# Attention with softmax, then a mixture of experts: PSUM banks moved from the row maxima to the scores, with another order of input chunks

## The reference

```python
x = L0_attn_x                                  # (4, 1024, 512), float32
x = layernorm(x + attention(x, wq, bq, wk, bk, wv, bv, wo, bo))   # 16 heads of 32
x = layernorm(x + ffn(x, ...))                 # 8 experts, top 2, and one shared expert

def attention(x, ...):
    q, k, v = x @ wq.T + bq, x @ wk.T + bk, x @ wv.T + bv         # split in 16 heads
    probs = softmax(q @ k.T / sqrt(32), axis=-1)                  # per batch and head, 1024 x 1024
    return (probs @ v) @ wo.T + bo
```

## Time and profile before

| | |
|---|---|
| median of three runs | 2168.53 us |
| the profiled execution | 2167.16 us |
| its span, first to last instruction | 2165.4 us |
| PE busy | 2053.6 us, 95% |
| DVE, ACT, POOL busy | 58%, 40%, 40% |
| mean granted clock of PE | 0.981 |

### The profile page before, as it was taken

The page is one execution under the profiler, slowest core; times in us unless marked ns, Lnnn a source line. Parts: engine busy times, 40 slices in busy tenths (PEclk is TensorE's granted clock), DMA queues, the critical chain, the costliest instruction groups (busy, mean ns, idle before and its releaser), DMA issues. The chain is left out here.

```text
span 2165.4 us, 29932 instructions
## 1 busy us (share of the span) xinstructions
PE 2053.6 (95%) x9636; PEld 1215.9 (56%) x9637; DVE 1265.8 (58%) x2247; ACT 866.7 (40%) x1530; POOL 869.7 (40%) x828
## 2 busy tenths in 40 slices
PE   7999899999899999899999987789999999999997
PEld 5655455555455555555555433468644444446886
DVE  5777676578676477677477753466222222224875
ACT  2265564366564266565266662321111111112332
POOL 2255564455554455655354554400011111113651
PEclk9999999999999999999999999899999999999999
DMA  5322333313333313333312302671222222224752
GB/s 165 69 50 64 84 75 88 113 37 77 84 74 83 118 31 77 91 75 80 122 28 58 79 12 93 214 282 52 85 88 87 89 94 89 87 82 148 228 179 73
DMA packets 94815, 205.90 MB, mean 95 GB/s; under 512 B 24608, under 2 KB 25120, under 8 KB 92256
## 3 DMA queue, kind: packets, MB, share of 16 engines
q1 hardware_dynamic: 83888, 168.90, 26.8%
q0 software_dynamic: 10800, 35.40, 5.9%
HBM read 113.53 MB, written 39.85 MB: 71 GB/s over the span
## 5 line engine op out<-in xcount | busy, mean ns | idle before, releaser
L852 DVE TENSOR_REDUCE max_half<-ps_side 128x1 f32<-128x512 f32 x1024 | 656.7, 682 | 235.4 <-PE ps_side L600 232.5
L768 ACT ACTIVATE probs_outer<-ps_s 128x512 f32<-128x512 f32 x629 | 365.3, 600 | 204.5 <-PE ps_s L622 173.6
L622 PE MATMUL ps_s<-kq_stack 97*128 97x512 f32 x937 | 399.2, 429 | 28.6 <-ACT probs_outer L768 21.4
L600 PE MATMUL ps_side<-kq_stack 96*128 96x512 f32 x1024 | 404.8, 404 | 2.9 <-DVE max_half L852 2.3
L622 PEld LDWEIGHTS ps_s<-kq_stack 97*128 97x128 f32 x937 | 179.4, 192 | 197.6 <-issue 98.3
L1516 PE MATMUL ps_gu<-gu_sb,xT_e 128*128 x568 | 257.7, 596 | 0.7 <-issue 0.5
L1414 POOL DMA_INDIRECT x_g<-x,who_all x71 | 67.4, 949 | 454.4 <-PE ps_t L1506 358.5
L600 PEld LDWEIGHTS ps_side<-kq_stack 96*128 96x128 f32 x1024 | 196.7, 192 | 53.0 <-DVE max_half L852 18.6
L768 ACT ACTIVATE probs_mid<-ps_s 128x512 f32<-128x512 f32 x308 | 178.4, 600 | 117.2 <-PE ps_s L622 102.2
L536 POOL TENSOR_TENSOR acc<-probs_outer,probs_mid 128x512 f32<-128x512 f32 x129 | 163.7, 1295 | 151.8 <-ACT probs_mid L768 151.8
L536 POOL TENSOR_TENSOR acc<-probs_outer 128x512 f32<-128x512 f32 x129 | 163.1, 1290 | 130.7 <-ACT probs_outer L768 130.7
(11 more groups left out here) (210 smaller groups left out, 3065.9 us busy)
## 6 DMA issues: line engine op xcount, KB each, us to landing
kq_stack<-kq SPq DMA_DIRECT2D x192, 256.0 KB, 5.1
y_slots<-y_t SPq DMA_DIRECT2D x71, 256.0 KB, 2.3
res<-inv_rows SPq DMA_DIRECT2D x128, 64.0 KB, 2.0
probs_outer<-x SPq DMA_DIRECT2D x16, 512.0 KB, 5.1
x_r<-x SPq DMA_DIRECT2D x32, 256.0 KB, 3.8
x_t<-x SPq DMA_DIRECT2D x32, 256.0 KB
gu_sb<-wgu SPq DMA_DIRECT2D x8, 1024.0 KB, 15.7
out<-gu_sb SPq DMA_DIRECT2D x32, 256.0 KB, 2.7
```

The lines of the kernel that those rows point to most:

```text
L600: nc.tensor.matmul(bank, q_stack[par][0:3 * HD, h, t * P:(t + 1) * P], k_stack[par][0:3 * HD, h, half * HALF:(half + 1) * HALF], start=Tru ...
L622: nc.tensor.matmul(out, k_stack[par][0:3 * HD + 1, h, kt * P:(kt + 1) * P], q_stack[par][0:3 * HD + 1, h, half * HALF:(half + 1) * HALF], ...
L768: nc.scalar.activation(probs(loc, h), score_bank(b, loc * HG + h)[0], ACT.Exp, scale=HD ** -0.5).then_inc(probs_ready, 1)
L852: nc.vector.reduce_max(max_half[:, u // 2, u % 2:u % 2 + 1], bank, AX.X).then_inc(side_free, 1)
```

## The change

- PSUM: pre and row units have two banks in turn in place of three. The bank that comes free (`SPARE`) is a third one for scores, from slot 3 of a batch on.
- Slots: one pre in each slot up to slot 62, with two in slot 28 only. Before they stopped after slot 60, and slots 12, 28 and 44 had two.
- The second row unit of a group (slot 63) comes behind `weighted` and `row_sums` on PE.
- Chunks of x: chunks 0 and 1 at the start of group 1 as before, chunks 2 and 3 between the transfers of `spread`, 4 and 5 at the start of group 2 ahead of `invert`, 6 and 7 behind the first `invert`. The rounding on ACT and the subtraction on POOL move to later steps, and the weights are loaded ahead of chunk 2.

```diff
-PRE_TWICE = (12, 28, 44)
-PRE_UNTIL = 61
+PRE_TWICE = (28,)
+PRE_UNTIL = 63
...
-X_HIGH = {(1, 8): 0, (1, 9): 1, (1, 10): 2, (1, 11): 3, (2, 1): 4, (2, 2): 5, (2, 4): 6, (2, 5): 7}
-X_AFTER = {(1, 9): (0,), (1, 11): (1, 2, 3), (2, 1): (4,), (2, 3): (5,), (2, 5): (6, 7)}
+X_HIGH = {(1, 8): (0, 1), (2, 0): (2,), (2, 1): (3,), (2, 4): (4,), (2, 5): (5,), (2, 7): (6,), (2, 8): (7,)}
+X_AFTER = {(1, 9): (0, 1), (2, 1): (2, 3), (2, 5): (4, 5), (2, 7): (6,), (2, 9): (7,)}
...
-SIDE_RING = 3
+SIDE_RING = 2
+SPARE, PROJ_BANK = RING + 2, RING + 3
...
+        if (g, slot) == (0, TAIL_RING - 1):
+            held[SPARE] = None
...
             def body(b, m, g, last):
-                x_chunks = g == 1 and not last
-                if x_chunks:
-                    load_x(b + 1, m + 3, range(2))
+                x_first_half, x_second_half = g == 1 and not last, g == 2 and not last
+                if x_first_half:
+                    load_x(b + 1, m + 3, (0, 1))
+                if x_second_half:
+                    load_x(b + 1, m + 2, (4, 5))
                 if g:
                     invert((b * G + g) * NHALF - 1)
+                if x_second_half:
+                    load_x(b + 1, m + 2, (6, 7))
...
-                if x_chunks:
-                    load_x(b + 1, m + 3, range(2, 4))
...
                 if not (last and g >= G - 2):
-                    spread(m + 2, g % 2, m)
+                    spread(m + 2, g % 2, m, {h: lambda i=h + 2: load_x(b + 1, m + 3, (i,))
+                                             for h in (0, 1)} if x_first_half else {})
                 if not (last and g == G - 1):
                     row(m, g, 1, last)
-                if x_chunks:
-                    load_x(b + 1, m + 3, range(4, CHUNKS))
...
+                        units = side_in(last, loc, slot)
+                        for kind, u, place in units:
+                            if kind != "row" or u == 0:
+                                side_unit(b, b * G + g, g, kind, u, place)
                         if slot == SLOTS - 1 and loc % FOLD == FOLD - 1:
...
                             row_sums(b, loc)
+                        for kind, u, place in units:
+                            if kind == "row" and u == 1:
+                                side_unit(b, b * G + g, g, kind, u, place)
```

More of the change, by code:

```diff
@@ L95, in score_banks @@
     banks, held, returned = [], {0: None, 1: None}, {}
-    proj = RING + SIDE_RING
+    proj = PROJ_BANK
     for i in range(G * STEPS * HG):
         g, slot = divmod(i - HG, STEPS * SLOTS)
+        if (g, slot) == (0, TAIL_RING - 1):
+            held[SPARE] = None
         if slot == LEND and not (last and g >= G - 2):
@@ L188, in attention @@
         ps_side = ctx.enter_context(nc.psum_tensor("ps_side", [P, TAIL_RING, HALF], F32))
-        ps_proj = ps_side[:, SIDE_RING, :]
+        ps_proj = ps_side[:, PROJ_BANK - RING, :]
         def score_bank(b, i):
@@ L246, in tail_bank @@
         def tail_bank(i):
-            return ps_side[:, (i + SIDE_RING) % TAIL_RING, :]
+            return ps_side[:, (i + TAIL_RING - 1) % TAIL_RING, :]
         def res_of(t):
@@ L311, in load_w @@
                     if g == 0:
-                        sp.wait_ge(x_split, (b + 1) * CHUNKS + 3 + sel)
+                        sp.wait_ge(x_split, (b + 1) * CHUNKS + 1 + sel)
                     elif g == 1:
@@ L323, in load_x @@
                         sp.wait_ge(w_split, 2 * (n - 1) + i + 1)
-                    elif i in (4, 5):
-                        sp.wait_ge(w_split, 2 * n + i - 3)
+                    elif i < 4:
+                        sp.wait_ge(w_split, 2 * n + i - 1)
                     else:
@@ L331, in load_x, with spread @@
                                      "a p t -> (a p) t")).then_inc(x_in[i % 2], 16)
-            def spread(n, par, m=None):
+            def spread(n, par, m=None, between={}):
                 sp.wait_ge(proj_free, PROJ * (n + 1))
@@ L343, in spread @@
                                      kq[h * HD:(h + 1) * HD, parts, :].bitcast(F32)).then_inc(stacked[h], 16)
+                    if h in between:
+                        between[h]()
             def send_rows(par, half):
@@ L617, in scores @@
                     pe.wait_ge(probs_ready, b * HEADS_B + before + 1)
-                elif bank == RING + SIDE_RING:
+                elif bank == PROJ_BANK:
                     pe.wait_ge(proj_free, PROJ * (b * G + (loc - 1) // STEPS + 3))
-                elif bank >= RING:
+                elif bank >= RING and bank != SPARE:
                     pe.wait_ge(side_free, base_of(B * G - 1))
@@ L672, in batch @@
                             scores(b, loc + 1, slot)
[L673 to L676, removed]
+                        if loc == 0 and slot < TAIL_RING - 1:
+                            pe.wait_ge(tail_free, b * TAIL + KT - (TAIL_RING - 2 - slot))
+                        units = side_in(last, loc, slot)
+                        for kind, u, place in units:
+                            if kind != "row" or u == 0:
+                                side_unit(b, b * G + g, g, kind, u, place)
                         if slot == SLOTS - 1 and loc % FOLD == FOLD - 1:
@@ L797, in batch @@
                             side_unit(b * G + g, g, kind, u, place)
-                    if (g, loc % STEPS) in X_HIGH and not last:
-                        x_part(b + 1, X_HIGH[g, loc % STEPS])
+                    for i in X_HIGH.get((g, loc % STEPS), ()) if not last else ():
+                        x_part(b + 1, i)
                     if loc % KT == KT - 1:
```

## The result

The changed kernel takes 2181.93 us (median of 6 runs, 2178.96 to 2186.17) against 2162.82 us of the kernel before (6 runs, 2160.02 to 2170.02): a ratio of 1.0085 [1.0064, 1.0106]. That is 19 us slower, inside the range of 2151 to 2192 and 6 us above the forecast of 2176.

The account below looks back on a forecast made before the run. PE, busy 95% of the span, was taken to bound the kernel. From the profiled 2167.2 us, minus 31 for late chunks, plus 39 for two maxima banks, gave 2175, or 2176 against the median; range 2151 to 2192 (8 in 10).

Parts of the forecast that it names:

- The late chunks go: Six long attention pairs in batches 0 to 2, where ACT waits for chunks of x: 31 us gained, 20 as lower end.
- What the third score bank brings: Scores waiting for ACT: beyond the six pairs little gain, as the other waits are at group ends, counted in pair 7.
- Two banks in ordinary pairs: Matmuls 0.09 us late for a bank, 0.19 us per ordinary pair; 2.2 us a group, 31 us over 14 groups.
- Pair 7: Last pair of a group, slots without proj: two banks follow DVE's pace, two pre more and one wait less, +0.37 us.
- Ahead of batch 0: Stretch before the first batch's attention, where DVE is nearly full as it is: +1.5 us.
- the last batch's group 2: Group without proj, every pair like pair 7: burst ends 0.6 us later, less what the doubles gave, +4.3 us.
- the boundaries: Between batches, products for v wait until DVE has copied the late row: 0.8 us in each of three.
- a change too small to tell: Whole kernel's time between 2157.7 and 2179.4 us, a change under 0.5%: chance 0.47.
- the next, slower: Whole kernel slower than 2179.4 us, from late chunks, the clock and the forecast's upper quarter: chance 0.33.
- The cheap ring: Rival on two maxima banks: half price, 1.0 us a group, 2157 us (0.16); almost nothing, 2145 us (0.12).
- The chunks don't stay late: Denies the rival that chunk 3 or 6 still stops ACT, 5 us a batch: 2191 us, or 2207; chance 0.16.
- The small gaps: Rival: twenty short PE waits in each group lower the granted clock, 3 us a group, 2218 us; chance 0.04.

## Why the prediction was right, and where it was off

- **The late chunks go, 31 us.** The pairs bear it out, −31.0 with the clock at 1.00, and chunk 6 is 1.0 us late, as predicted. The cause was named too narrowly: the new order alone brings 23 us. What the third score bank brings "beyond that is little", I wrote. With three banks for maxima the new places of the chunks cost 5.3 us without it, with two they cost 3.5, and even in the old order it gives 0.81 us in the pair looked at.
- **Two banks in ordinary pairs, 0.09 us at a time.** From the three times of the rows came +0.10, −0.05, +0.19, +0.65, +0.40 and +0.55 for pairs 0 to 5; measured +0.08, −0.01, +0.13, +0.70, +0.38 and +0.59. (Pair 2 is +0.19 where it was undisturbed; in the three groups with late chunks it had been 8.39 and lost 0.12.) Three banks again give 8.09 for pair 1 and 8.20 for pair 5, so the ring is the cause. The release of a bank 0.84 us after its maximum began was read from one row and carried.
- **Pair 7, the step that failed: +0.37 predicted, +1.0 in nine of eleven.** I followed the burst of pres and the products with v to the row behind the sums, and took the sums as free. They wait for DVE's fold. Before, it starts 4.00 us into the pair, while POOL's last fold runs, and all eleven pairs take the short way; the longer burst of pres pushes it to 4.56, and there POOL mostly goes straight on to normalise. The two pairs that went the short way show 7.51, +0.37, so the burst itself was worked out rightly. This is 5.6 us of the 11 that were missed.
- **Ahead of batch 0: +1.5 predicted, +5.3 measured.** The term was a guess and not worked from rows. Before, DVE is busy for 19.4 of the 20 us from 50 to 70, and PE for 19.0. With two banks PE runs into DVE 11 times, both do less (17.6 and 17.9 of the 20 us), and from 40 us to the first pair 10.2 us are at 1.2 GHz in place of 6.8. This is 3.8 us of the 11. Of the rest, 0.9 is the last batch's group 2 (+5.2 for +4.3), and 0.5 the boundaries.
- **Where the luck was.** The time came out 6 us above the forecast, and the slowdown 11.6 above it; the other 5.7 us are the first three runs of the kernel before, which lay high. The prediction's likeliest outcome, a change too small to tell (0.47), isn't what came, but the next, slower (0.33).
- **The rivals.** The cheap ring is out: the changed kernel is 51 us above the same with three banks for maxima. (Its sum was off: 14 × 1.0 and the 8.2 outside make 22 us and not 20, the time 2159.) The chunks don't stay late. The small gaps didn't pull the clock down: it is 1.00 in every window of an ordinary pair, and the mean rises from 0.981 to 0.985.
- **Two of 14 pairs 4 took 9.2 us** in place of 8.57: DVE waits 0.85 us for the transfer of `sum_few` ahead of the reciprocal in slot 36, with the maxima behind it. With three banks both stand at 8.18.

```profile
337.29:346.51 9.22, 8.54 (x50) 4.45 (x46) 6.42 (x10) 5.05 (x9) 5.02 (x4) 1.00 0.05 11
```
```profile
342.29 0.25 DVE L880 RECIPROCAL inv_few<-sum_few 128x16 f32<-128x16 f32 x1 [0.85 <-DMA sum_few<-res]
```

## What to carry to other kernels

Before taking a buffer from a ring, work out the release time from a row (producer's start to consumer's start, and to when the buffer may be filled again) and lay it against the pace slot by slot: delays of 0.1 us show in no wait of the engine, only in its weight loads and in the distance between like places, and here pairs 0 to 6 made half of the 50 us lost, while PE shows 9 us of idle time in them. Price each half of a change with and without the other, since a buffer that hides a wait can be a part of what the other half seems to bring (here up to 8 of 31 us). And where a stage gets longer, list everything that the next one waits for, here a fold on another engine, not only the chain that was looked at.

## What the runs showed of the hardware that I had not expected

DVE's sum of two arrays in SBUF, 128x512, takes 0.68 us in the 47 of the changed kernel's 136 folds that overlap no POOL instruction, and up to 2.42 us in the other 89 (2.58 with three banks for maxima). It isn't slowed in proportion: in all these 89 it ends 0.55 to 0.63 us behind the end of a POOL instruction. Which of the two comes next when both stand waiting isn't fixed: the same program point went either way within one execution, nine times to two in the changed kernel, and three times to eight with three banks ahead of batch 0. It hangs on hundredths of a microsecond. I took the ten pairs 7 of batches 0 to 2 and of batch 3's group 0 in each of the five traces where DVE's fold starts at 4.56 (two banks and the new slots, with POOL's normalising behind step 15). Where POOL's second fold started 2.65 us or more into the pair, 20 of 21 went the long way; where it started up to 0.01 us sooner, 9 of 29. What decides it stays open.
